# Per-chunk waits in the FFN groups, statistics straight from fp32 x, and PSUM banks of their own for the LayerNorm broadcasts

## The chip, the cores and the metric

The kernel runs on one Trainium2 chip, the same program on all 8 NeuronCores, each on its own batch element of 2048 tokens. No core talks to another. The time is that of the slowest core, in microseconds (us).

## What is computed

A macaron layer: half an FFN, attention, half an FFN, each on a LayerNorm of x and added back to x. The model width is 1024. The FFN is one shared expert and two routed ones, all with a hidden width of 4096; a token goes to one routed expert by argmax of a two-row gate.

```python
def _L0_attn_ref(x, wq, bq, wu, bu):          # 16 heads of 64
    q = x @ wq.T + bq
    qh = q.reshape(HEADS, b, s, hd)           # keys and values are qh too
    attn = softmax(qh @ qh^T * scale)
    return (attn @ qh).reshape(b, s, emb) @ wu.T + bu

def _L0_ffn_ref(x, ...):
    top1 = argmax(softmax(xf @ gate_w.T))
    masked = xf * one_hot(top1)               # one copy per routed expert
    routed = sum_e(relu(masked_e @ w1_e + b1_e) @ w2_e + b2_e)
    shared = relu(xf @ sw1 + sb1) @ sw2 + sb2
    return routed + shared

x = x + 0.5 * ffn(layernorm(x))
x = x + attn(layernorm(x))
x = x + 0.5 * ffn(layernorm(x))
```

## The kernel before

x lies transposed and in fp32 in `x_sb` (128 partitions, 8 chunks `kc` of the width, 2048 tokens) for the whole run. Tokens are cut into 4 strips `st` of 512. The hidden width of the three experts is cut into 12 pieces `sup` of 1024: 0 to 3 are the shared expert (class 0), 4 to 7 and 8 to 11 the routed ones (classes 1 and 2). The loop is over `sup`, within it over `st`: each of these 48 steps of an FFN, called a step below, is `do_mm1` and then `do_mm2` (L535, L578). The weights of the next `sup` are fetched by the POOL queue into the other of two slots.

`do_mm1` makes 8 groups `hc` of 8 matmuls (L552) in turn into PSUM banks `ps_a` and `ps_b`; ScalarE takes each group through ReLU into its part of `ar_h` (L562). The right-hand side is the LayerNorm output `ar_ln` for class 0, and for the routed classes a masked copy `ar_b` of 8 chunks. The 8 masked chunks of the next step are made by VectorE (L524), one behind each of the 8 evacuations of the present `do_mm2` (`pending_lnm`). `do_mm2` makes 8 groups `dc` of 8 matmuls (L586) in turn into `ps_c` and `ps_d`; VectorE adds each to `x_sb` (L606, for `sup` 0 L599).

Each engine runs its instructions in the order in which the program emits them. Order between engines is kept by counting semaphores, one per producing engine: `sch.wait("tensor", DVE, n)` holds everything behind it on TensorE until VectorE has done n counted operations. Before the change, the first matmul of `do_mm1` waits for all 8 chunks, and the first of `do_mm2` for all 8 parts of `ar_h` (`h_all`).

LayerNorm works by strip in two stages. `stage_stats` (L308): VectorE casts a chunk of x to bf16 into a one-strip scratch (L325), TensorE sums it over partitions by a matmul with a column of ones (L333, one output row), 8 times in turn through that one scratch; then ScalarE squares a chunk into the same scratch (L347) and TensorE sums it (L355), 8 times in turn; VectorE writes both rows (L340, L362). `stage_post` (L367): on one row, variance (L377, L379), square root on ScalarE (L386), reciprocal (L391); TensorE spreads both rows over 128 partitions with two fp32 matmuls (L400, L404), VectorE copies them out (L410, L412) and normalises 8 chunks with two operations each (L422, L426), through the scratch. `stage_gate` (L432) makes the routing masks.

In an FFN these stages are written into the steps of `sup` 0: stats 0, stats 1, post 0, then for each strip `do_mm1`, stats of strip st+2, post of strip st+1, `do_mm2`, and the gates from strip 2 on. `do_mm2` of `sup` 0 waits for all that VectorE has been given so far (`mm2_extra`), because the broadcasts and gates use `ps_c` and `ps_d` too; `ext["bc_wait"]` guards the same banks from the other side. In attention, `emit_ln` (L492) writes stats 0, stats 1, post 0, stats 2, post 1, stats 3, post 2, post 3; then `qproj` (L895) waits for all of it (`ln_done`).

Of the kernel before, what the change touches and what calls it, by code (L numbers as in the profile page):

```python
# [12 lines left out]
NT = 2048  # L13
# [55 lines left out]
def build(phases=("ffn1", "attn", "ffn2")):  # L69
# [15 lines left out]
    with es:  # L85
# [14 lines left out]
        ones_col = sb("ones_col", [128, 1], BF16)  # L100
        onesLf = sb("onesLf", [1, 128], F32)
# [188 lines left out]
        def make_ln_stages(is_ffn, xwaits, statps, bcps, ext=None):  # L290
# [7 lines left out]
            bcev = [0] * NSTRIP  # L298

# [8 lines left out]
            def stage_stats(st):  # L308
                t0 = st * TS
                xb = scratch(st)  # L310
# [4 lines left out]
                sch.wait("vector", DVE, max(xwaits[st], tok_b2))  # L315
                sch.wait("scalar", DVE, max(xwaits[st], tok_b2))
                prev_mm = statmm[st - 1] if st > 0 else 0
                sch.wait("vector", X, tok_xload)
                if st >= 2:
                    sch.wait("vector", DVE, ln_tok[st - 2])  # L320
                for kc in range(NKC):
                    sch.wait("vector", MM, prev_mm)
                    sch.wait("vector", ACTs, sqtok[st - 2] if st >= 2 else 0)
                    def fcast(v, S, _kc=kc, _t0=t0, _xb=xb):
                        v.tensor_copy(  # L325
                            _xb[:, :], x_sb[:, _kc * NT + _t0: _kc * NT + _t0 + TS]
                        ).then_inc(S[DVE], 1)
                    sch.emit("vector", fcast)
                    ctok = sch.bump(DVE, 1)
                    sch.wait("tensor", GP, tok_gpinit)  # L330
                    sch.wait("tensor", DVE, max(ctok, s1ev[st - 1] if st >= 1 else 0))
# [6 lines left out]
                sch.wait("vector", MM, s1mm)  # L338
                def fs1(v, S, _sp=sp1, _r=r1):
                    v.tensor_scalar_mul(_r, _sp, 1.0 / D).then_inc(S[DVE], 1)  # L340
                sch.emit("vector", fs1)
                s1ev[st] = sch.bump(DVE, 1)
                for kc in range(NKC):
                    sch.wait("scalar", MM, prev_mm)
                    sch.wait("scalar", X, tok_xload)
# [7 lines left out]
                    sch.wait("tensor", DVE, s2ev[st - 1] if st >= 1 else 0)  # L353
# [4 lines left out]
                    prev_mm = sch.bump(MM, 1)  # L358
                statmm[st] = prev_mm
# [7 lines left out]
            def stage_post(st):  # L367
# [34 lines left out]
                bct1 = sch.bump(MM, 1)  # L402
                def fbc2(t, S, _r=r2, _bp=bB):
# [11 lines left out]
                xb = scratch(st)  # L415
                sch.wait("vector", DVE, bcev[st])
                sch.wait("vector", ACTs, sqtok[st])
                for kc in range(NKC):
                    base_n = sch.val(DVE)
                    def fn(v, S, _kc=kc, _t0=t0, _b=base_n, _xb=xb, _mB=mB, _sB=sB):  # L420
                        v.wait_ge(S[DVE], _b)
                        v.tensor_sub(_xb[:, :],  # L422
# [3 lines left out]
                        v.tensor_mul(ln_ap(_kc, _t0, TS), _xb[:, :],  # L426
                                     _sB[:, :]).then_inc(S[DVE], 1)
                    sch.emit("vector", fn)
                    ln_tok[st] = sch.bump(DVE, 2)


            def stage_gate(st):  # L432
# [4 lines left out]
                for e in range(2):  # L437
                    gp_ps = bcps[e]
                    for kc in range(NKC):
                        sch.wait("tensor", *tok_gw)  # L440
                        sch.wait("tensor", DVE, ln_tok[st])
                        sch.wait("tensor", DVE, ext.get("bc_wait", 0))
# [14 lines left out]
                    gevac = sch.bump(DVE, 1)  # L457
                sch.wait("vector", DVE, gevac)
# [9 lines left out]
                sch.wait("tensor", DVE, mrow_tok)  # L468
                bB2 = bcps[1]
# [15 lines left out]
                mask_tok[st] = sch.bump(DVE, 2)  # L485

# [17 lines left out]
        def emit_ffn(xwait_dve, wst, ps_d, ps_w, ps_w2):  # L504
            ext = {"bc_wait": 0}
# [8 lines left out]
            lnm_tok = [None]  # L514

            pending_lnm = []

            def build_lnm_pieces(st, klass, wait_mm):
                which = 0 if klass == 1 else 1
                def piece(kc):  # L520
# [6 lines left out]
                    lnm_tok[0] = sch.bump(DVE, 1)  # L527
                return [lambda _kc=kc: piece(_kc) for kc in range(NKC)]
# [6 lines left out]
            def do_mm1(sup, st, klass, slot):  # L535
# [80 lines left out]
            for st in range(NSTRIP):  # L616
                do_mm1(0, st, 0, 0)
                ext["bc_wait"] = sch.val(DVE)
# [12 lines left out]
            for st in (2, 3):  # L631
                ext["bc_wait"] = sch.val(DVE)
                gf[st]()
            ps2_free[0] = ps2_free[1] = sch.val(DVE)
# [18 lines left out]
        def emit_attn(xwait_dve, s0, s1, d_att, ps_t, ps_rz, hooks):  # L653
# [106 lines left out]
            def av_row(i, a):  # L760
                if a == 0:
                    sch.wait("tensor", DVE, state["avfree"])
# [132 lines left out]
            def qproj(half):  # L895
                t0h = half * 1024
                qev = [0, 0]
                for dc in range(NKC):
                    for st2 in range(2):
# [3 lines left out]
                        sch.wait("tensor", DVE, max(ln_done, state["avfree"],  # L903
# [67 lines left out]
        if do1:  # L971
            with nc.psum_tensor("ps_d1", [128, TS], F32) as ps_d1, \
                 nc.psum_tensor("ps_w1", [1, TS], F32) as ps_w1, \
                 nc.psum_tensor("ps_v1", [1, TS], F32) as ps_v1:
# [11 lines left out]
                xw, _, ffn1_mm = emit_ffn(0, wst1, ps_d1, ps_w1, ps_v1)  # L986
# [26 lines left out]
        if do2:  # L1013
            with nc.psum_tensor("ps_d2", [128, TS], F32) as ps_d2, \
                 nc.psum_tensor("ps_w2", [1, TS], F32) as ps_w2, \
                 nc.psum_tensor("ps_v2", [1, TS], F32) as ps_v2:
# [13 lines left out]
                _, xtok, _ = emit_ffn(xw, wst2, ps_d2, ps_w2, ps_v2)  # L1030
# [97 lines left out]
```

## Time and profile before

| what | us |
|---|---|
| median of the 2 runs shown | 4909.22 (4900.01 to 4918.43) |
| the profiled execution, its own time | 4656.95 |
| its span on the slowest core (core 6) | 4655.4 |
| the other cores' spans | 4630.0 to 4653.5 |
| FFN 1, attention, FFN 2 within the span | about 50 to 1731, 1731 to 2980, 2980 to the end |

The profiled execution is 252 us shorter than the median of the runs. Busy time of TensorE matmuls on core 6 is 3826.6 us (82%), of VectorE 1235.9 us (27%), of ScalarE 1221.7 us (26%). In the rows, PE is TensorE, PEld its weight loads, DVE VectorE, ACT ScalarE. PEclk or "clock" is the granted TensorE clock as a share of full speed. A row of the timeline gives start, duration, engine, line, operation, output<-inputs, a count, and in brackets the idle time before it and what ended that. The end of the last matmul of a merged row is modelled: a row of 8 lasts 1.89 us, while the next begins 1.73 us after its start.

### The profile page before, as it was taken

Reading aid. Unit: us, or ns where it says so; the run is one execution under the profiler, and the core shown is the slowest. Engines: PE = TensorE matmul, PEld = TensorE weight load, DVE = VectorE, ACT = ScalarE, POOL = GpSimd, SP = SyncE. Lnnn points to the kernel's source line nnn. Section 1 sums busy time; section 2 is a strip of 40 time slices with the busy share of each in tenths; the row PEclk is TensorE's granted clock in tenths of the full one; section 3 lists DMA queues with packets and bytes.
Section 4 is the critical chain, followed back from the end, with each engine's and each line's share of the span. In section 5 each row is a group of like instructions: output and inputs, shape, how many; then the busy total and the mean of one; then the engine's idle time right before and its main releaser. Section 6 shows DMA issues by size and latency. Waiting matters only on the chain. (4 is left out here: it accounts for less than half of the span.)

```text
span 4655.4 us, 45328 instructions; the slowest of 8 cores (4630.0 to 4655.4 us)
## 1 busy us (share of the span) xinstructions
PE 3826.6 (82%) x16529; PEld 1583.2 (34%) x16784; DVE 1235.9 (27%) x2311; ACT 1221.7 (26%) x2945; POOL 48.5 (1%) x66
## 2 busy tenths in 40 slices
PE   1568999999999983588888888655899999999998
PEld 0223444444444430123333333222344444444443
DVE  2342112222222224411222222234211222222222
ACT  1111111111111111266664666311111111111111
POOL 0000000000000000000000000000000000000000
PEclk9778899999999995656566656667999999999999
DMA  7002222222221100100001000300222222222101
GB/s 145 0 0 37 37 37 37 37 37 37 37 35 30 28 1 0 18 1 1 1 1 19 1 1 1 55 0 0 37 37 37 37 37 37 37 37 32 30 12 73
DMA packets 55268, 124.61 MB, mean 27 GB/s; under 512 B 1808, under 2 KB 1808, under 8 KB 53008
## 3 DMA queue, kind: packets, MB, share of 16 engines
q0 software_dynamic: 52144, 104.86, 14.6%
q1 hardware_dynamic: 2912, 16.85, 1.1%
q8 instruction: 142, 2.33, 0.2%
q14 instruction: 70, 0.57, 0.0%
HBM read 218.18 MB, written 8.39 MB: 49 GB/s over the span
## 5 line engine op out<-in xcount | busy, mean ns | idle before, releaser
L586 PE MATMUL ps_c<-ar_h,ar_w 128*128 128x512 bf16 x3009 | 735.9, 385 | 177.3 <-DVE ar_ln L426 88.2
L562 ACT ACTIVATE ar_h<-ps_a,b1hf 128x512 bf16<-128x512 f32 x384 | 263.8, 687 | 2188.7 <-PE ps_a L552 2188.7
L586 PE MATMUL ps_d<-ar_h,ar_w 128*128 128x512 bf16 x3012 | 729.7, 383 | 3.3
L606 DVE TENSOR_TENSOR x_sb<-x_sb,ps_c 128x512 f32<-128x512 f32 x352 | 242.0, 687 | 1712.4 <-PE ps_c L586 1712.4
L552 PE MATMUL ps_a<-ar_b,ar_w 128*128 128x512 bf16 x2010 | 482.0, 380 | 88.8 <-DVE ar_b L524 86.9
L586 PEld LDWEIGHTS ps_c<-ar_h,ar_w 128*128 128x128 bf16 x3072 | 297.1, 99 | 575.4 <-issue 256.3
L552 PE MATMUL ps_b<-ar_b,ar_w 128*128 128x512 bf16 x2004 | 480.7, 380 | 2.3
L741 PE MATMUL s<-ar_h 64*128 64x512 bf16 x768 | 413.9, 566 | 74.8 <-ACT ar_w L752 54.5
L586 PEld LDWEIGHTS ps_d<-ar_h,ar_w 128*128 128x128 bf16 x3072 | 303.2, 99 | 371.5 <-issue 29.1
L562 ACT ACTIVATE ar_h<-ps_b,b1hf 128x512 bf16<-128x512 f32 x384 | 263.8, 687 | 412.6 <-PE ps_b L552 410.8
L752 ACT ACTIVATE ar_w<-s 128x512 bf16<-128x512 f32 x432 | 255.0, 599 | 285.7 <-PE s L741 285.2
L606 DVE TENSOR_TENSOR x_sb<-x_sb,ps_d 128x512 f32<-128x512 f32 x352 | 242.0, 688 | 288.6 <-PE ps_d L586 288.6
L552 PEld LDWEIGHTS ps_a<-ar_b,ar_w 128*128 128x128 bf16 x2048 | 196.1, 98 | 343.9 <-issue 117.8
L552 PEld LDWEIGHTS ps_b<-ar_b,ar_w 128*128 128x128 bf16 x2048 | 200.8, 98 | 242.8 <-issue 2.1
L552 PE MATMUL ps_a<-ar_ln,ar_w 128*128 128x512 bf16 x993 | 252.8, 396 | 31.9 <-DVE rzb_sb L325 14.9
L552 PE MATMUL ps_b<-ar_ln,ar_w 128*128 128x512 bf16 x1011 | 251.1, 391 | 0.6
L524 DVE TENSOR_TENSOR ar_b<-ar_ln,ar_b 128x512 bf16<-128x512 bf16 x512 | 212.8, 418 | 0.0
L741 PEld LDWEIGHTS s<-ar_h 64*128 64x128 bf16 x768 | 74.8, 103 | 363.0 <-issue 361.9
L552 PEld LDWEIGHTS ps_a<-ar_ln,ar_w 128*128 128x128 bf16 x1024 | 102.9, 101 | 163.1 <-issue 63.9
L741 PE MATMUL ps_t<-ar_h 64*128 64x512 bf16 x256 | 147.8, 577 | 4.8
L552 PEld LDWEIGHTS ps_b<-ar_ln,ar_w 128*128 128x128 bf16 x1024 | 103.0, 101 | 129.8 <-issue 29.7
L752 ACT ACTIVATE ar_ln<-s 128x512 bf16<-128x512 f32 x176 | 105.3, 614 | 42.8 <-PE s L741 42.8
(172 smaller groups left out, 2533.5 us busy)
## 6 DMA issues: line engine op xcount, KB each, us to landing
ar_w<-w1c POOLq DMA_DIRECT2D x24, 2048.0 KB, 18.1
ar_w<-w2c POOLq DMA_DIRECT2D x24, 2048.0 KB, 29.0
x_sb<-x SPq DMA_DIRECT2D x1, 8192.0 KB, 37.8
y<-x_sb SPq DMA_DIRECT2D x8, 1024.0 KB, 8.7
ar_w<-wqt POOLq DMA_DIRECT2D x1, 2048.0 KB, 16.7
ar_w<-wut POOLq DMA_DIRECT2D x1, 2048.0 KB, 16.4
b1hf<-b1h SPq DMA_DIRECT2D x1, 48.0 KB, 39.8
bq_sb<-bqc SPq DMA_DIRECT2D x1, 4.0 KB, 40.9
```

Source lines behind the costliest of these rows:

```text
L524: v.tensor_mul(lnm_ap(_kc), ln_ap(_kc, _st * TS, TS), mask_ap(_w, _st)).then_inc(S[DVE], 1)
L552: ins = t.matmul(_pst[:, :], w1blk(_slot, _kc, _hc), _rhs(_kc), start=(_kc == 0), stop=(_kc == NKC - 1))
L562: s.activation(ar_h[:, _hc * TS:(_hc + 1) * TS], _pst[:, :], AF.Relu, bias=b1hf[:, _sup * 8 + _hc:_sup * 8 + _hc + 1], scale=0.5).then_inc ...
L586: ins = t.matmul(_pst[:, :], w2blk(_slot, _hc, _dc), ar_h[:, _hc * TS:(_hc + 1) * TS], start=(_hc == 0), stop=(_hc == NKC - 1))
L606: v.tensor_add(xsl, xsl, _pst[:, :]).then_inc(S[DVE], 1)
L741: t.matmul(_sr[:, :], qq_ap(_pa, _h), ar_h[_h:_h + 64, _q4 * TS:(_q4 + 1) * TS], start=True, stop=True).then_inc(S[MM], 1)
L752: s.activation(prow_ap(_a)[:, _q4 * TS:(_q4 + 1) * TS], _sr[:, :], AF.Exp, scale=SCALE, accum_out=_z[:, _a * 4 + _q4:_a * 4 + _q4 + 1]).th ...
```

## The change

- The sum of x is taken by fp32 matmuls directly from `x_sb` with a column of fp32 ones; the 8 casts of a strip and their waits go.
- The squares alternate between two scratch tiles (`xb_s`, `xb2`), each with its own wait.
- Normalisation writes straight into `ar_ln` and scales it there; the scratch is not used. Each chunk's count is kept (`ln_ktok`), and so is each masked chunk's (`lnm_ktok`).
- The first group of `do_mm1` waits chunk by chunk, and the first group of `do_mm2` waits part by part of `ar_h`.
- The FFN's broadcasts and gates get two banks of their own, `ps_e` and `ps_f`, each with its own release (`bfree`). `bc_wait` and the wait of `sup` 1 for the gates go. `mm2_extra` stays.
- `qproj` waits for the strip it reads, and `av_row` takes over the wait for all of LayerNorm.

```diff
@@ stage_stats
-                xb = scratch(st)
...
-                prev_mm = statmm[st - 1] if st > 0 else 0
-                sch.wait("vector", X, tok_xload)
-                if st >= 2:
-                    sch.wait("vector", DVE, ln_tok[st - 2])
+                sch.wait("tensor", GP, tok_gpinit)
+                sch.wait("tensor", X, tok_xload)
+                sch.wait("tensor", DVE, max(xwaits[st], tok_b2,
+                                            s1ev[st - 1] if st >= 1 else 0))
                 for kc in range(NKC):
-                    sch.wait("vector", MM, prev_mm)
-                    sch.wait("vector", ACTs, sqtok[st - 2] if st >= 2 else 0)
-                    def fcast(v, S, _kc=kc, _t0=t0, _xb=xb):
-                        v.tensor_copy(
-                            _xb[:, :], x_sb[:, _kc * NT + _t0: _kc * NT + _t0 + TS]
-                        ).then_inc(S[DVE], 1)
-                    sch.emit("vector", fcast)
-                    ctok = sch.bump(DVE, 1)
...
-                    def fmm(t, S, _kc=kc, _sp=sp1, _xb=xb):
-                        t.matmul(_sp, ones_col[:, :], _xb[:, :],
+                    def fmm(t, S, _kc=kc, _t0=t0, _sp=sp1):
+                        t.matmul(_sp, ones_colf[:, :],
+                                 x_sb[:, _kc * NT + _t0: _kc * NT + _t0 + TS],
                                  start=(_kc == 0), stop=(_kc == NKC - 1)).then_inc(S[MM], 1)
...
                 for kc in range(NKC):
-                    sch.wait("scalar", MM, prev_mm)
-                    sch.wait("scalar", X, tok_xload)
+                    xb = xb_s if kc % 2 == 0 else xb2
+                    sch.wait("scalar", MM, sq_mm_last[kc % 2])
...
+                    sq_mm_last[kc % 2] = prev_mm
@@ stage_post
-                sch.wait("tensor", DVE, ext.get("bc_wait", 0))
-                if st >= 1:
-                    sch.wait("tensor", DVE,
-                             mask_tok[st - 1] if is_ffn else bcev[st - 1])
+                sch.wait("tensor", DVE, bfree[0])
...
+                sch.wait("tensor", DVE, bfree[1])
...
-                        v.tensor_sub(_xb[:, :],
+                        v.tensor_sub(ln_ap(_kc, _t0, TS),
                                      x_sb[:, _kc * NT + _t0: _kc * NT + _t0 + TS],
                                      _mB[:, :]).then_inc(S[DVE], 1)
                         v.wait_ge(S[DVE], _b + 1)
-                        v.tensor_mul(ln_ap(_kc, _t0, TS), _xb[:, :],
+                        v.tensor_mul(ln_ap(_kc, _t0, TS), ln_ap(_kc, _t0, TS),
                                      _sB[:, :]).then_inc(S[DVE], 1)
...
+                    ln_ktok[st][kc] = ln_tok[st]
@@ emit_ffn
-                (ps_w[:, :], ps_w2[:, :]), (ps_d[:, :], ps_c[:, :]), ext)
+                (ps_w[:, :], ps_w2[:, :]), (ps_e[:, :], ps_f[:, :]), ext)
@@ do_mm1
-                    sch.wait("tensor", rhs_sem, rhs_tok)
+                    if hc > 0:
+                        sch.wait("tensor", rhs_sem, rhs_tok)
                     for kc in range(NKC):
+                        if hc == 0:
+                            sch.wait("tensor", rhs_sem, rhs_ktok[kc])
@@ do_mm2
-                    sch.wait("tensor", ACTs, h_all)
+                    if dc > 0:
+                        sch.wait("tensor", ACTs, h_all)
                     for hc in range(NKC):
+                        if dc == 0:
+                            sch.wait("tensor", ACTs, h_relu_tok[hc])
@@ emit_ffn, after sup 0
-            ps2_free[0] = ps2_free[1] = sch.val(DVE)
@@ qproj
-                        sch.wait("tensor", DVE, max(ln_done, state["avfree"],
+                        sch.wait("tensor", DVE, max(ln_tok[half * 2 + st2],
+                                                    state["avfree"],
                                                     state["ufree"]))
```

How the instructions move is shown at two places. First TensorE in a step of a routed class, from the last group of one `do_mm2` (ps_d) through `do_mm1` (ps_a, ps_b) to the first group of its `do_mm2` (ps_c). Before:

```order
L586 MATMUL ps_d<-ar_h,ar_w 128x512 [waits s_dve]
L586 MATMUL ps_d<-ar_h,ar_w 128x512 x7
L552 MATMUL ps_a<-ar_b,ar_w 128x512 [waits s_dve]
L552 MATMUL ps_a<-ar_b,ar_w 128x512 x7
L552 MATMUL ps_b<-ar_b,ar_w 128x512 x8
...
L552 MATMUL ps_b<-ar_b,ar_w 128x512 x7
L586 MATMUL ps_c<-ar_h,ar_w 128x512 [waits s_act]
L586 MATMUL ps_c<-ar_h,ar_w 128x512 x7
```

The same place in the changed kernel:

```order
L599 MATMUL ps_d<-ar_h,ar_w 128x512 [waits s_dve]
L599 MATMUL ps_d<-ar_h,ar_w 128x512 x7
L562 MATMUL ps_a<-ar_b,ar_w 128x512 x5
L562 MATMUL ps_a<-ar_b,ar_w 128x512 [waits s_dve] x3
L562 MATMUL ps_b<-ar_b,ar_w 128x512 x8
...
L562 MATMUL ps_b<-ar_b,ar_w 128x512 x7
L599 MATMUL ps_c<-ar_h,ar_w 128x512 x6
L599 MATMUL ps_c<-ar_h,ar_w 128x512 [waits s_act] x2
```

Five matmuls of `do_mm1` now stand ahead of the first wait for VectorE (the waits of those five are already covered by an earlier one), and six of `do_mm2` ahead of the first wait for ScalarE; the matmuls themselves and their order are unchanged.

Second TensorE in stats 0 and the first of stats 1 of the first FFN (ps_w takes the sums of x, ps_v those of the squares; rzb_sb and p_ex are the two scratch tiles). Before:

```order
L333 MATMUL ps_w<-rzb_sb,ones_col 1x512 [waits s_gp,s_dve]
L333 MATMUL ps_w<-rzb_sb,ones_col 1x512 [waits s_dve] x7
L355 MATMUL ps_v<-rzb_sb,ones_col 1x512 [waits s_act] x8
L333 MATMUL ps_w<-p_ex,ones_col 1x512 [waits s_dve] x8
L355 MATMUL ps_v<-p_ex,ones_col 1x512 [waits s_act] x8
```

And in the changed kernel:

```order
L326 MATMUL ps_w<-x_sb,ones_colf 1x512 [waits s_gp,s_x,s_dve]
L326 MATMUL ps_w<-x_sb,ones_colf 1x512 x7
L353 MATMUL ps_v<-rzb_sb,ones_col 1x512 [waits s_act]
L353 MATMUL ps_v<-p_ex,ones_col 1x512 [waits s_act]
...
L326 MATMUL ps_w<-x_sb,ones_colf 1x512 [waits s_dve]
L326 MATMUL ps_w<-x_sb,ones_colf 1x512 x7
```

The 8 sums of x have one wait at their head instead of one each and read `x_sb`; the sums of the squares keep a wait each but alternate between the two scratch tiles.

## Rows read from the trace of the kernel before

**Rows 1.** the page: busy time, share of the span and instructions of each engine

```profile
PE 3826.6 (82%) x16529; PEld 1583.2 (34%) x16784; DVE 1235.9 (27%) x2311; ACT 1221.7 (26%) x2945; POOL 48.5 (1%) x66
```

**Rows 2.** waits, core 6: who waited for whom, us in total, times, longest

```profile
PE ps_c L586 <- DVE ar_ln L426: 88.2, 6, 14.9
PE ps_a L552 <- DVE ar_b L524: 86.9, 64, 3.6
PE ps_c L586 <- ACT ar_h L562: 85.9, 90, 1.4
```

**Rows 3.** timeline, one step of class 1: TensorE, VectorE, ScalarE

```profile
3764.41 1.89 PE L586 MATMUL ps_d<-ar_h,ar_w 128*128 128x512 bf16 x8
3767.57 1.89 PE L552 MATMUL ps_a<-ar_b,ar_w 128*128 128x512 bf16 x8 [1.28 <-DVE ar_b L524]
3779.66 1.89 PE L552 MATMUL ps_b<-ar_b,ar_w 128*128 128x512 bf16 x8
3782.47 1.89 PE L586 MATMUL ps_c<-ar_h,ar_w 128*128 128x512 bf16 x8 [0.93 <-ACT ar_h L562]
...
3766.40 0.69 DVE L606 TENSOR_TENSOR x_sb<-x_sb,ps_d 128x512 f32<-128x512 f32 x1 [0.71 <-PE ps_d L586]
3767.01 0.42 DVE L524 TENSOR_TENSOR ar_b<-ar_ln,ar_b 128x512 bf16<-128x512 bf16 x1
...
3781.64 0.69 ACT L562 ACTIVATE ar_h<-ps_b,b1hf 128x512 bf16<-128x512 f32 x1 [1.04 <-PE ps_b L552]
```

**Rows 4.** timeline, first LayerNorm of FFN 1: stats and post of strip 0

```profile
50.66 0.58 PE L333 MATMUL ps_w<-rzb_sb,ones_col 128*1 128x512 bf16 x1 [50.66 <-DVE rzb_sb L325]
...
71.85 0.68 DVE L362 TENSOR_SCALAR ar_b<-ps_v 1x512 f32<-1x512 f32 x1 [10.95 <-PE ps_v L355]
...
94.19 0.68 DVE L362 TENSOR_SCALAR p_ex<-ps_v 1x512 f32<-1x512 f32 x1 [10.95 <-PE ps_v L355]
...
100.76 2.04 PE L400 MATMUL ps_d<-ar_b,onesLf 1*128 1x512 f32 x2 [6.68 <-DVE ar_b L391]
102.60 1.91 PE L404 MATMUL ps_c<-ar_b,onesLf 1*128 1x512 f32 x2
...
119.05 3.57 PE L552 MATMUL ps_a<-ar_ln,ar_w 128*128 128x512 bf16 x8 [14.54 <-DVE ar_ln L426]
```

**Rows 5.** timeline, TensorE where class 1 begins

```profile
3668.53 1.89 PE L586 MATMUL ps_d<-ar_h,ar_w 128*128 128x512 bf16 x8
3674.04 3.57 PE L552 MATMUL ps_a<-ar_b,ar_w 128*128 128x512 bf16 x8 [3.62 <-DVE ar_b L524]
```

**Rows 6.** timeline, TensorE and VectorE: stats 2 in FFN 1

```profile
134.91 0.38 PE L333 MATMUL ps_w<-rzb_sb,ones_col 128*1 128x512 bf16 x1
...
155.04 0.68 DVE L362 TENSOR_SCALAR ar_b<-ps_v 1x512 f32<-1x512 f32 x1 [10.95 <-PE ps_v L355]
```

**Rows 7.** timeline, TensorE: the gate of strip 2 in FFN 1

```profile
371.05 3.57 PE L444 MATMUL ps_d<-ar_ln,gw_bf 128*1 128x512 bf16 x8 [1.74 <-DVE ar_b L483]
374.41 2.50 PE L444 MATMUL ps_c<-ar_ln,gw_bf 128*1 128x512 bf16 x8
```

**Rows 8.** timeline, TensorE and VectorE: LayerNorm of attention

```profile
1732.34 0.38 PE L333 MATMUL s<-rzb_sb,ones_col 128*1 128x512 bf16 x1 [2.06 <-DVE rzb_sb L325]
...
1776.72 0.68 DVE L362 TENSOR_SCALAR p_ex<-s 1x512 f32<-1x512 f32 x1 [10.95 <-PE s L355]
...
1823.29 0.68 DVE L362 TENSOR_SCALAR ar_b<-s 1x512 f32<-1x512 f32 x1 [10.95 <-PE s L355]
...
1919.46 2.87 PE L908 MATMUL ps_a<-ar_ln,ar_w 128*128 128x512 bf16 x7 [14.92 <-DVE ar_ln L426]
```

**Rows 9.** windows, core 6: busy us of PE, PEld, DVE, ACT, POOL, granted clock, DMA

```profile
400.00:500.00 100.00, 96.50 (x362) 39.85 (x369) 16.52 (x24) 15.11 (x22) 0.00 (x0) 0.81 0.21 34
800.00:900.00 100.00, 92.91 (x420) 41.45 (x428) 24.54 (x48) 20.31 (x30) 1.76 (x2) 1.00 0.11 16
```

**Rows 10.** the same view, core 0

```profile
400.00:500.00 100.00, 95.81 (x436) 43.04 (x444) 19.94 (x29) 18.34 (x27) 0.00 (x0) 1.00 0.18 27
```

More of the change, by code:

```diff
@@ L100, in build @@
         ones_col = sb("ones_col", [128, 1], BF16)
+        ones_colf = sb("ones_colf", [128, 1], F32)
         onesLf = sb("onesLf", [1, 128], F32)
@@ L184, in g_init @@
             g.memset(ones_col[:, :], 1.0)
+            g.memset(ones_colf[:, :], 1.0)
             g.memset(onesLf[:, :], 1.0)
@@ L298, in make_ln_stages @@
             bcev = [0] * NSTRIP
+            bfree = [0, 0]
+            sq_mm_last = [0, 0]
+            ln_ktok = [[0] * NKC for _ in range(NSTRIP)]
+            ext["ln_ktok"] = ln_ktok
             def tiles(st):
@@ L338, in stage_stats @@
                 sch.wait("vector", MM, s1mm)
+                sch.wait("vector", DVE, ln_tok[st - 2] if st >= 2 else 0)
                 def fs1(v, S, _sp=sp1, _r=r1):
@@ L342, in stage_stats @@
                 s1ev[st] = sch.bump(DVE, 1)
+                sch.wait("scalar", DVE, max(xwaits[st], tok_b2))
+                sch.wait("scalar", X, tok_xload)
                 for kc in range(NKC):
-                    sch.wait("scalar", MM, prev_mm)
-                    sch.wait("scalar", X, tok_xload)
+                    xb = xb_s if kc % 2 == 0 else xb2
+                    sch.wait("scalar", MM, sq_mm_last[kc % 2])
                     def fsq(s, S, _kc=kc, _t0=t0, _xb=xb):
@@ L352, in stage_stats @@
                     sch.wait("tensor", ACTs, sqtok[st])
-                    sch.wait("tensor", DVE, s2ev[st - 1] if st >= 1 else 0)
+                    if kc == 0:
+                        sch.wait("tensor", DVE, s2ev[st - 1] if st >= 1 else 0)
                     def fmm2(t, S, _kc=kc, _sp=sp2, _xb=xb):
@@ L414, in stage_post, with fn @@
                 bcev[st] = sch.bump(DVE, 2)
-                xb = scratch(st)
+                bfree[0] = bcev[st] - 1
+                bfree[1] = bcev[st]
                 sch.wait("vector", DVE, bcev[st])
-                sch.wait("vector", ACTs, sqtok[st])
                 for kc in range(NKC):
                     base_n = sch.val(DVE)
-                    def fn(v, S, _kc=kc, _t0=t0, _b=base_n, _xb=xb, _mB=mB, _sB=sB):
+                    def fn(v, S, _kc=kc, _t0=t0, _b=base_n, _mB=mB, _sB=sB):
                         v.wait_ge(S[DVE], _b)
-                        v.tensor_sub(_xb[:, :],
+                        v.tensor_sub(ln_ap(_kc, _t0, TS),
                                      x_sb[:, _kc * NT + _t0: _kc * NT + _t0 + TS],
@@ L441, in stage_gate @@
                         sch.wait("tensor", DVE, ln_tok[st])
-                        sch.wait("tensor", DVE, ext.get("bc_wait", 0))
+                        sch.wait("tensor", DVE, bfree[e])
                         def fg(t, S, _e=e, _kc=kc, _t0=t0, _sp=gp_ps):
@@ L457, in stage_gate @@
                     gevac = sch.bump(DVE, 1)
+                    bfree[e] = gevac
                 sch.wait("vector", DVE, gevac)
@@ L468, in stage_gate @@
                 sch.wait("tensor", DVE, mrow_tok)
+                sch.wait("tensor", DVE, max(bfree[0], bfree[1]))
                 bB2 = bcps[1]
@@ L485, in stage_gate @@
                 mask_tok[st] = sch.bump(DVE, 2)
+                bfree[0] = mask_tok[st] - 1
+                bfree[1] = mask_tok[st]
             stats_fns = [lambda _st=st: stage_stats(_st) for st in range(NSTRIP)]
@@ L502, in emit_ln, with emit_ffn @@
             return ln_tok, mask_tok
-        def emit_ffn(xwait_dve, wst, ps_d, ps_w, ps_w2):
-            ext = {"bc_wait": 0}
+        def emit_ffn(xwait_dve, wst, ps_d, ps_w, ps_w2, ps_e, ps_f):
+            ext = {}
             sf, pf, gf, ln_tok, mask_tok = make_ln_stages(
                 True, [xwait_dve] * NSTRIP,
-                (ps_w[:, :], ps_w2[:, :]), (ps_d[:, :], ps_c[:, :]), ext)
+                (ps_w[:, :], ps_w2[:, :]), (ps_e[:, :], ps_f[:, :]), ext)
+            ln_ktok = ext["ln_ktok"]
             h_relu_tok = [0] * NKC
@@ L514, in emit_ffn @@
             lnm_tok = [None]
+            lnm_ktok = [0] * NKC
             pending_lnm = []
@@ L542, in do_mm1 @@
                     rhs = lambda kc, _t0=st * TS: ln_ap(kc, _t0, TS)
+                    rhs_ktok = [ln_ktok[st][kc] for kc in range(NKC)]
                 else:
@@ L545, in do_mm1 @@
                     rhs = lambda kc: lnm_ap(kc)
+                    rhs_ktok = list(lnm_ktok)
                 for hc in range(NKC):
@@ L761, in av_row @@
                 if a == 0:
-                    sch.wait("tensor", DVE, state["avfree"])
+                    sch.wait("tensor", DVE, max(state["avfree"], ln_done))
                 sch.wait("tensor", ACTs, state["exp_tok"][(i, a, 3)])
@@ L973, in build @@
                  nc.psum_tensor("ps_w1", [1, TS], F32) as ps_w1, \
-                 nc.psum_tensor("ps_v1", [1, TS], F32) as ps_v1:
+                 nc.psum_tensor("ps_v1", [1, TS], F32) as ps_v1, \
+                 nc.psum_tensor("ps_e1", [128, TS], F32) as ps_e1, \
+                 nc.psum_tensor("ps_f1", [128, TS], F32) as ps_f1:
                 for s0 in range(2):
@@ L1015, in build @@
                  nc.psum_tensor("ps_w2", [1, TS], F32) as ps_w2, \
-                 nc.psum_tensor("ps_v2", [1, TS], F32) as ps_v2:
+                 nc.psum_tensor("ps_v2", [1, TS], F32) as ps_v2, \
+                 nc.psum_tensor("ps_e2", [128, TS], F32) as ps_e2, \
+                 nc.psum_tensor("ps_f2", [128, TS], F32) as ps_f2:
                 if wst2["w1"][0] is None:
```

14 lines of the change are left out of this document (3 added, 11 removed).

## The prediction

> **What bounds the kernel now.** I read the page first. TensorE is busy for 82% of the span, no other engine for more than 27% [rows 1]. A kernel like that gains only where TensorE stands still or runs at a lower clock, so the second view is the list of waits, cut down to those of TensorE [rows 2]. Three lines stand out, and the change aims at two. 85.9 us go in 90 waits of the first group of `do_mm2` for the ReLU on ScalarE, 86.9 us in 64 waits of the first group of `do_mm1` for the masked chunks of VectorE. The third, 88.2 us in 6 waits of about 14.7 us, is `do_mm2` of `sup` 0 waiting until the next strip is normalised.
>
> The third view is the timeline of one step [rows 3]. Groups of 8 matmuls begin 1.73 us apart, 0.216 us a matmul. The last `ps_d` group begins at 3764.41, so the next group could begin at 3766.14; it begins at 3767.57, 1.43 us late. In between stand the evacuation of `ps_d` (from 3766.40, 0.69 us) and the eighth masked chunk (3767.01, 0.42 us, done at 3767.43). The last `ps_b` group begins at 3779.66, its follower could begin at 3781.39 and begins at 3782.47, 1.08 us late, behind a ReLU that ends at 3782.33. All the earlier chunks and parts were ready long before. That is 2.5 us beside 128 x 0.216 = 27.6 us of matmuls, a step of 30.2.
>
> LayerNorm is the rest. In the first one TensorE's first sum begins at 50.66 and the second row of strip 0 is written at 71.85, that of strip 1 at 94.19: 21.8 us (from the cast that starts 0.6 before 50.66) and 22.3 us for the statistics of a strip of 512 tokens. In them one scratch tile is passed to and fro between engines. Post of strip 0 ends where the first group begins, at 119.05, about 24.2 us after that second row [rows 4].
>
> **Step 1, the first group of `do_mm2`.** The wait for all eight parts becomes one per part. The eighth matmul would start 7 x 0.216 = 1.51 us after 3781.39, at 3782.90, and its part is ready at 3782.33, plus the 0.14 us that the hand-over to 3782.47 took. The other seven cover it with 0.4 us to spare. Gain 1.08 x 90 = 97 us [rows 2, 3]. Below this, the idle time itself bounds it, 86 us.
>
> **Step 2, the first group of `do_mm1`.** Of the 64 waits, 62 are as in [rows 3]. The eighth matmul would start at 3766.14 + 1.51 = 3767.65, the chunk is handed over at 3767.57. This cover is thin: 0.08 us. A matmul that has waited starts right behind its weight load, which could cost up to one place of 0.216 us. I take 0.05 us: 62 x 1.38 = 86 us, between 75 and 89. The other two are where a class begins with nothing prepared [rows 5]: TensorE is 3.78 us late (3670.26 to 3674.04), and its first group then takes 3.57 us at the half clock. With waits by chunk that group ends soon after the last chunk. 2 x 4 = 8 us, at least 2.
>
> **Step 3, statistics in the FFNs.** 8 casts and 8 hand-overs go; 8 fp32 matmuls on 128 partitions come, which the trace does not show. The nearest rows are the fp32 broadcasts: 102.60 - 100.76 = 1.84 us for one with 512 columns [rows 4]. That was at the half clock: the group of 8 bf16 matmuls behind it lasts 3.57 us in place of the 1.89 of [rows 3]. At full clock I estimate half of that, 0.92 us. So a pass of 8 is 14.7 us at the half clock and 7.4 at full. Dense matmuls with a single output row ran while the clock rose: 8 of them took 3.36 us from 371.05, and the next 8 last 2.50 us [rows 7]. So behind an idle stretch I take a value between the ends, nearer the fast one: 9.3 us. The squares now run in two tiles; two are ready when the fp32 pass ends, and the other six come at ScalarE's pace, at most the 0.69 us of a ReLU of the same size [rows 3] and 0.1 of hand-over, about 5.3 us to the second row. That is 14.6 us for strips 0 and 1 against 21.8 and 22.3: 7 + 7.5. Strips 2 and 3 follow a warm `do_mm1`: 7.4 + 5.3 = 12.7 us against 155.04 - 134.91 = 20.1 [rows 6]: 7.4 each. The first `do_mm1` follows normalisation chunk by chunk and its group of 3.57 us shrinks to one matmul's length: 3 us. Together 32 us an FFN, 65 for both. If the fp32 pass stays at the half clock it is 14.7 + 5.8 = 20.5 us a strip, and of the 65 only 10 are left. Upper end 70. The other part of the LayerNorm chain is not shortened: `do_mm2` still waits for everything given to VectorE, so the 88 us of the third line in [rows 2] stay. Writing into `ar_ln` in place has the same two operations as before and costs nothing.
>
> **Step 4, LayerNorm of attention.** Before, the casts of strip 2 stood on VectorE behind the normalisation of strip 0, so nothing overlapped: 46.6 us a strip (1823.29 - 1776.72), and 188 us in all from a cast about 0.4 us before 1732.34 to 1919.46 [rows 8]. Now statistics need VectorE for two rows only. Stats of strips 2 and 3 run on TensorE and ScalarE while VectorE normalises. A post stage is 46.6 - 22.3 = 24.3 us, as in the FFN. New sum: 13 + 14.6 for the first two statistics, 4 x 24.3, and 2 x 1.6 for the rows of the other two: 128 us. Gain 60. With a slow fp32 pass the statistics (20.5 us) no longer fit behind a post stage, of which some 14.5 us are left after its broadcasts: 41 + 97 + 12 = 150, gain 38. `qproj` may start its first two groups before the last strip is done; two PSUM banks and VectorE, busy normalising, hold it there, so I count nothing and keep 4 us for the upper end.
>
> **Step 5, banks of their own.** The gates no longer wait for the mask copies of the one before (1.74 us idle at 371.05 [rows 7]). About 1 us for each of 8 gates: 8 us, from 4 to 12.
>
> **Sum.** 97 + 86 + 8 + 65 + 60 + 8 = 324 us. The profiled execution took 4656.95, so its like would take 4333. The median of the runs is 4909.22, 252 us more; the removed waits are fixed hand-overs between engines, so I take the same 324 off: 4585. From the bounds, 4560 to 4690.
>
> **Rival A, the clock gives it back (slower).** Core 6 ran 400 to 500 at a granted clock of 0.81, neither of the two levels of 1.2 and 2.4 GHz, while core 0 on the other die had 1.00 with the same work [rows 9, 10]. It fell in the densest stretch (96.5 us busy of 100), and was 1.00 where every step had the wait for the masked chunks (92.9). The change makes all steps as dense as that. At 0.81 a matmul takes 0.216/0.81 = 0.266 us, 0.05 more. Two FFNs have 2 x 48 x 128 = 12,288 of them: 614 us, less some 30 that core 6 has already paid, 584. The gain is gone once 324/0.05 = 6,500 matmuls, 53%, run so. The time would be 4657 - 324 + 584 = 4917 if the 252 us above the profile are already this, and 5169 if they are not. Against it: core 0 was as dense and kept 1.00, and both kernels pass through the dense stretch.
>
> The Trainium skill, TensorE: Matmul & The Clock Gate, section Seeing it yourself, says that a peak-current limit takes a die to 13/16 of the clock when three of its cores run dense matmuls, and holds it while the load lasts. By that rule both kernels should be held there in all of the FFNs. The trace shows the level (0.81) but not the rule: only for a part of the time and on part of the cores.
>
> **Rival B, fp32 passes stay slow and the eighth wait binds.** All lower ends: 97 + 75 + 2 + 10 + 38 + 4 = 226 us, 4683. For it: the first sum lasts 0.58 us where the first of stats 2, behind dense work, lasts 0.38 [rows 4, 6], so sparse statistics leave the clock low.
>
> **Rival C, the runs fall to the profile's level.** The same gain at the clock of the profiled execution: 4335. For it speaks only that the profiled execution was there.
>
> **Rival D, the waits move and don't shrink.** Then the change does not do what it says: waits one by one stop TensorE as long as one wait did, steps 1 and 2 give nothing, and 65 + 60 + 8 + 8 = 141 us are left: 4768. Against it, [rows 3]: the earlier chunks are ready before the group begins.
>
> **How the numbers follow.** The forecast has 0.62, A 0.12, B 0.14, C 0.08, D 0.04. A measurement of this kernel tells about 2% from no change, that is 98 us. The forecast, B, C and D are all faster by more than that, 0.88; of A I put 0.07 within 2% and 0.05 slower; I give the first 0.87 and the middle 0.08. The range leaves out A and C and holds the rest with the mixed cases between: 4400 to 4850.
>
> **What would show it.** In the profile after: the two waits of [rows 2] at under 10 us each, and routed steps of 27.7 us instead of 30.2. If steps stay over 29 us, step 2 is wrong. An fp32 sum's pitch near 0.92 us within stats of strips 2 and 3 confirms step 3; 1.84 there means B. In attention, `qproj` should begin about 130 us after the last evacuation of FFN 1. A granted clock near 0.81 in the routed steps, on more than half of the FFN time, means A, and then the time misses upwards though every wait is gone.

## The result and the profile after

| | before | changed |
|---|---|---|
| median of all runs | 4721.57 (10 runs, 4634.19 to 5054.93) | 4551.65 (11 runs, 4289.92 to 4801.87) |
| undisturbed runs, mean of 5 | 4648.5 (4634.2 to 4658.6) | 4308.8 (4289.9 to 4314.2) |
| profiled execution, its span | 4656.95, 4655.4 | 4315.33, 4313.7 |

The changed kernel is faster: ratio 0.9269, 95% interval 0.9235 to 0.9304, in undisturbed runs 340 us. "Undisturbed" leaves out the runs in which the cores of one die, at times of both, were granted a lower clock and took longer (in one run of the changed kernel cores 0 to 3 had 0.76 and took up to 4827 us, cores 4 to 7 had 0.867 and took at most 4289). Forecast were 324 us of gain, a time of 4585 and a range from 4400. The gain is right to 5%, the time is not: the undisturbed time lies 276 us below the forecast and 90 below the range.

The page, busy time of each engine:

```profile
PE 3842.3 (89%) x16880; PEld 1602.4 (37%) x16880; DVE 1194.8 (28%) x2215; ACT 1217.3 (28%) x2945; POOL 48.5 (1%) x67
```

TensorE's busy time is within 16 us of that in [rows 1]; the span shrank around it. VectorE lost 41 us, the casts. The waits on core 7, the slowest (us in total, times, longest):

```profile
PE ps_c L599 <- DVE ar_ln L423: 87.6, 6, 14.9
```

and the group of the page that holds the waits of `do_mm1` (busy, mean ns, idle before it):

```profile
L562 PE MATMUL ps_a<-ar_b,ar_w 128*128 128x512 bf16 x2048 | 485.8, 379 | 2.8 <-DVE ar_b L528 2.6
```

Of the three lines of [rows 2] the one for `ar_ln` stays at 6 waits and 88 us. The one for masked chunks fell from 86.9 to 2.6 us, and `ps_c` has none for `ar_h` any more. One step of a routed class, core 7, the place that answers to [rows 3]:

```profile
3484.44 1.89 PE L599 MATMUL ps_c<-ar_h,ar_w 128*128 128x512 bf16 x8
...
3496.52 1.89 PE L599 MATMUL ps_d<-ar_h,ar_w 128*128 128x512 bf16 x8
3498.25 1.89 PE L562 MATMUL ps_a<-ar_b,ar_w 128*128 128x512 bf16 x8
...
3510.34 1.89 PE L562 MATMUL ps_b<-ar_b,ar_w 128*128 128x512 bf16 x8
3512.06 1.89 PE L599 MATMUL ps_c<-ar_h,ar_w 128*128 128x512 bf16 x8
...
3498.52 0.69 DVE L619 TENSOR_TENSOR x_sb<-x_sb,ps_d 128x512 f32<-128x512 f32 x1 [0.35 <-PE ps_d L599]
3499.13 0.42 DVE L528 TENSOR_TENSOR ar_b<-ar_ln,ar_b 128x512 bf16<-128x512 bf16 x1
```

From `ps_c` to `ps_c` 27.62 us, which is 128 x 0.216 and nothing more. The last chunk is made while the group that reads it already runs: it ends at 3499.55, which with the hand-over of 0.14 us of the prediction makes 3499.69, and the eighth matmul is due at 3498.25 + 1.51 = 3499.76.

LayerNorm of FFN 1, TensorE on core 0, the place of [rows 4]:

```profile
48.37 10.00 PE L326 MATMUL ps_w<-x_sb,ones_colf 128*1 128x512 f32 x16 [48.37 <-DVE b2sh L241]
58.21 0.38 PE L353 MATMUL ps_v<-rzb_sb,ones_col 128*1 128x512 bf16 x1
...
62.68 7.03 PE L326 MATMUL ps_w<-x_sb,ones_colf 128*1 128x512 f32 x16
69.55 0.38 PE L353 MATMUL ps_v<-rzb_sb,ones_col 128*1 128x512 bf16 x1
...
80.86 2.04 PE L396 MATMUL ps_e<-ar_b,onesLf 1*128 1x512 f32 x2 [6.67 <-DVE ar_b L390]
...
149.48 3.57 PE L599 MATMUL ps_c<-ar_h,ar_w 128*128 128x512 bf16 x8 [14.54 <-DVE ar_ln L423]
```

The 8 fp32 sums (16 records) take 9.84 us from 48.37 and 6.87 from 62.68, the 8 squares behind them 4.47. The broadcasts begin 32.5 us after the first sum; before they began 50.1 us after it [rows 4]. The last row is one of the six waits that stay.

Attention's LayerNorm, TensorE on core 0 and one row of VectorE, the place of [rows 8]:

```profile
1571.82 7.03 PE L326 MATMUL s<-x_sb,ones_colf 128*1 128x512 f32 x16 [1.27 <-PEq L1057]
...
1601.54 2.04 PE L396 MATMUL ps_c<-ar_b,onesLf 1*128 1x512 f32 x2 [6.67 <-DVE ar_b L390]
...
1605.22 9.82 PE L326 MATMUL s<-x_sb,ones_colf 128*1 128x512 f32 x16
...
1618.99 0.69 DVE L423 TENSOR_TENSOR ar_ln<-ar_ln,ar_b 128x512 bf16<-128x512 bf16 x1
1619.14 0.38 PE L353 MATMUL s<-p_ex,ones_col 128*1 128x512 bf16 x1
...
1676.72 2.04 PE L396 MATMUL ps_c<-p_ex,onesLf 1*128 1x512 f32 x2 [20.27 <-DVE p_ex L390]
...
1680.80 3.19 PE L916 MATMUL ps_a<-ar_ln,ar_w 128*128 128x512 bf16 x7 [0.33 <-issue]
1683.78 2.97 PE L916 MATMUL ps_b<-ar_ln,ar_w 128*128 128x512 bf16 x8
1696.04 3.57 PE L916 MATMUL ps_a<-ar_ln,ar_w 128*128 128x512 bf16 x8 [9.28 <-DVE ar_b L925]
```

The sums of strip 2 (from 1605.22) run while VectorE normalises strip 0, so the post stages, 25 us apart, set the pace. They only just do: the last sum of squares of strip 2 starts at 1619.14, and the last operation of the normalisation ends at 1618.99 + 0.69 = 1619.68. Longer statistics would show. Two groups of `qproj` are made while the last strip is normalised, and the third waits for an evacuation behind that.

Core 0 of both profiled executions, cut at the first matmul of each part:

| part | before | changed | difference |
|---|---|---|---|
| FFN 1, LayerNorm and class 0 | 688.4 | 636.6 | -51.9 |
| FFN 1, routed classes | 968.3 | 886.9 | -81.4 |
| attention, LayerNorm and qproj | 217.4 | 151.3 | -66.0 |
| attention, the rest | 1032.3 | 1031.5 | -0.8 |
| FFN 2, LayerNorm and class 0 | 693.3 | 630.2 | -63.1 |
| FFN 2, routed classes | 981.3 | 899.5 | -81.8 |

These add to 345 us on core 0 (spans 4630.0 and 4284.3).

### The profile page after: what moved, and what is told of

It is laid out like the page before. It is cut to its first block and busy times, and to the rows that moved or that the text cites. A ratio compares the mean times of both kernels' runs of the same rounds, so it can differ in the third digit from the quotient of the medians.

```text
span 4313.7 us, 45734 instructions; the slowest of 8 cores (4284.3 to 4313.7 us)
## 1 busy us (share of the span) xinstructions
PE 3842.3 (89%) x16880; PEld 1602.4 (37%) x16880; DVE 1194.8 (28%) x2215; ACT 1217.3 (28%) x2945; POOL 48.5 (1%) x67
## 5 line engine op out<-in xcount | busy, mean ns | idle before, releaser
L599 PE MATMUL ps_c<-ar_h,ar_w 128*128 128x512 bf16 x3072 | 741.5, 385 | 87.6 <-DVE ar_ln L423 87.6
```

Of the source, the lines that this page charges most:

```text
L599: ins = t.matmul(_pst[:, :], w2blk(_slot, _hc, _dc), ar_h[:, _hc * TS:(_hc + 1) * TS], start=(_hc == 0), stop=(_hc == NKC - 1))
```

## The experiments

The time of an experiment is that of its fastest run, beside the fastest run of its reference on the same chip; the fastest two or three runs of one kernel mostly lie within 4 us of each other. "Theory" in the expectations is the sum of the prediction at the lower level, with its terms by part.

### One part alone

`e1_mm2_only` is the kernel before with the waits of `do_mm2` split:

```diff
-                    sch.wait("tensor", ACTs, h_all)
+                    if dc > 0:
+                        sch.wait("tensor", ACTs, h_all)
                     for hc in range(NKC):
+                        if dc == 0:
+                            sch.wait("tensor", ACTs, h_relu_tok[hc])
```

> Step 1 alone on the kernel before: the first group of do_mm2 waits part by part. If the eighth ReLU is covered by seven matmuls, the 90 waits of 1.08 us go and no other wait grows: 97 us less than before, routed steps of 29.1 us. Rival (the waits only move): the ReLU wait reappears before the eighth matmul or in front of do_mm1, and the time stays within 10 us of before.

Measured: 4541.4 against 4635.4, 94 us off, ratio 0.9798 (0.9769 to 0.9826); a routed step takes 29.06 us on core 0, where the kernel before takes 30.15. Its waits on core 0:

```profile
PE ps_c L589 <- DVE ar_ln L426: 88.0, 6, 14.9
PE ps_a L552 <- DVE ar_b L524: 86.8, 64, 3.6
```

Exactly one line of [rows 2] is gone and the other two are unchanged: the idle time was removed, not moved.

`e2_mm1_only` is the kernel before with the same edit in `do_mm1` (and the counts it needs):

```diff
-                    sch.wait("tensor", rhs_sem, rhs_tok)
+                    if hc > 0:
+                        sch.wait("tensor", rhs_sem, rhs_tok)
                     for kc in range(NKC):
+                        if hc == 0:
+                            sch.wait("tensor", rhs_sem, rhs_ktok[kc])
```

> Step 2 alone on the kernel before: the first group of do_mm1 waits chunk by chunk. If the cover of 0.08 us holds: 94 us less than before (62 waits of 1.4 us, two of 4, and up to 3 us in each first do_mm1 behind a LayerNorm: 100). Rival (the eighth wait binds and costs a weight load): 75 to 80 us less, with a gap of about 0.2 us before the eighth matmul in 62 steps.

Measured: 4531.0, 104 us off, ratio 0.9777 (0.9735 to 0.9819). A steady routed step takes 28.72 us on core 0 for 30.15, the whole 1.43 us of the late start, so the thin cover of the eighth matmul holds.

`e3_ln_only` is the changed kernel with both waits put back (the two edits above reversed), so that steps 3 to 5 are alone.

> The changed kernel with both waits of the steps put back, so LayerNorm, gates and banks alone. If the parts add up: what is left of the 340 us between the fast runs after 97 and 94, about 149 us less than before. Rival (the LayerNorm part is worth only my lower ends, 52 us, and the two step waits give more than their price because TensorE keeps its clock): under 100 us less.

Measured: 4488.9, 147 us off, ratio 0.9685 (0.9657 to 0.9713). The three parts add to 94 + 104 + 147 = 345, the whole measured 340 (the means of the first table) to 346 (the fastest runs, on different chips): no interaction shows.

### The statistics

The next three ran beside the changed kernel on another chip (`a1_after_again`, 4289.3).

> The changed kernel once more, as the mark for the other three on this chip: 340 us less than before if the level at which both are compared is that of the undisturbed runs (4649 and 4309), 324 by my sum.

`e7_sums_twice` makes the fp32 sums of every strip twice; `start` restarts the sum, so the output is the same.

```diff
-                for kc in range(NKC):
+                for kc in list(range(NKC)) * 2:
                     def fmm(t, S, _kc=kc, _t0=t0, _sp=sp1):
```

> The changed kernel with every fp32 sum of x made twice (the second time over the same accumulator, so the row is unchanged). It prices the fp32 pass: 8 matmuls of 0.86 us more in each of the 8 strips of the FFNs and the first 2 of attention, 69 us, and 0 to 14 us in the other 2 of attention, which lie beside a normalisation: 70 to 85 us more than the changed kernel. Rival (the pass is hidden behind ScalarE's squares): under 30 us more.

Measured: 4374.7, in a single run, 85 us more. Against the profiled execution of the changed kernel the LayerNorm part of FFN 1 grew on core 0 by 28 us, of FFN 2 by 31 and of attention by 26. TensorE there:

```profile
48.22 15.55 PE L326 MATMUL ps_w<-x_sb,ones_colf 128*1 128x512 f32 x32 [48.22 <-DVE b2sh L241]
...
68.08 13.89 PE L326 MATMUL ps_w<-x_sb,ones_colf 128*1 128x512 f32 x32
```

The second pass costs 13.73 - 6.87 = 6.86 us at full clock, 0.858 us per matmul of 512 columns, 12 times 82 us. All of it is on the path, in attention too, where I had thought that two of the four strips hide it: the rows of attention above show that the statistics of strip 2 end together with the normalisation beside them, so nothing is left to hide a second pass.

`e4_bf16_casts` takes the sums of x from bf16 casts again, but through the two scratch tiles in turn:

```diff
+                    xb = xb_s if kc % 2 == 0 else xb2
+                    sch.wait("vector", MM, sq_mm_last[kc % 2])
...
+                        v.tensor_copy(
+                            _xb[:, :], x_sb[:, _kc * NT + _t0: _kc * NT + _t0 + TS]
...
-                        t.matmul(_sp, ones_colf[:, :],
-                                 x_sb[:, _kc * NT + _t0: _kc * NT + _t0 + TS],
+                        t.matmul(_sp, ones_col[:, :], _xb[:, :],
```

> The changed kernel with the sums of x taken from bf16 casts on VectorE again, but through both scratch tiles in turn. If fp32 is worth having only where it frees VectorE: statistics in the FFNs get a little shorter (8 casts of 0.43 us in place of 8 sums of 0.86, the first squares no longer ready beforehand), about 15 us less over both FFNs, while in attention the casts of strips 2 and 3 stand behind a normalisation again, 20 us more. In all within 20 us of the changed kernel. Rival (fp32 itself is the gain): 40 us or more above it.

Measured: 4304.5, 15 us more; the profiled execution took 4324.4, and on cores 4 to 7 at most 4298. In it the LayerNorm part of FFN 1 is 7 to 16 us shorter on all cores. That of FFN 2 is 629.6 us on cores 4 to 7, where the changed kernel takes 630.2 at its best; on cores 0 to 3 it is 23 to 25 us longer, at a lower granted clock. Attention's is 20 (core 0) to 22 us (cores 5 to 7) longer. Attention, strip 2, core 0:

```profile
1609.84 0.58 PE L334 MATMUL s<-rzb_sb,ones_col 128*1 128x512 bf16 x1 [14.87 <-DVE rzb_sb L327]
...
1615.09 0.58 PE L361 MATMUL s<-rzb_sb,ones_col 128*1 128x512 bf16 x1 [0.44 <-ACT rzb_sb L352]
```

TensorE waits 14.87 us for a cast that stands on VectorE behind a strip's normalisation. So in the FFNs fp32 buys nothing beside the second tile; it pays in attention, because it takes VectorE out of the statistics. The fp32 sums with a single scratch tile were not run. The rows also show the spaced sums at the half clock (0.58 us, where the rows behind an fp32 pass have 0.38).

### The 88 us that stayed

`e5_no_extra` takes away the wait of `do_mm2` of `sup` 0 for everything given to VectorE (`mm2_extra`), which own banks make needless:

```diff
-                do_mm2(0, st, 0, sch.val(DVE))
+                do_mm2(0, st, 0, 0)
```

> The changed kernel without the wait of do_mm2 of sup 0 for all that VectorE was given (mm2_extra). TensorE can then make two groups into ps_c and ps_d while VectorE normalises, and waits for the evacuations after that: 3 to 5 us in each of 6 places, 20 to 30 us less than the changed kernel. Rival (this wait is the whole of the 88 us): 80 us less.

Measured: 4278.4, 11 us less where 20 to 30 were expected. A miss; TensorE on core 0 shows why:

```profile
134.16 3.59 PE L599 MATMUL ps_c<-ar_h,ar_w 128*128 128x512 bf16 x8
137.54 2.90 PE L599 MATMUL ps_d<-ar_h,ar_w 128*128 128x512 bf16 x8
149.43 3.57 PE L599 MATMUL ps_c<-ar_h,ar_w 128*128 128x512 bf16 x8 [8.99 <-DVE x_sb L612]
```

and its waits have, in place of the 87.6 us for `ar_ln`:

```profile
PE ps_c L599 <- DVE x_sb L612: 58.1, 6, 10.2
```

Two groups start early, at the half clock. The third needs `ps_c` back, whose evacuation stands on VectorE behind the normalisation, and after 9 us of idling it is at the half clock too (3.57). So of the 29.5 us of idle time that went, much came back as slow matmuls: here the two groups took 6.3 us (134.16 to 149.43 less 8.99) that take 3.45 at full clock. In the six places 1.8 to 2.8 us were lost so, 13 in all, and the groups behind the wait took 3 us more in all than in the changed kernel. That leaves 13 of 29.5, near the 11 measured.

`e6_post_in_mm1` therefore moves the cause. The row part of post is emitted ahead of `do_mm1` of `sup` 0, its broadcasts and normalisation behind the fourth group of it, and the extra wait goes; in attention the rows of strips 2 and 3 stand ahead of the normalisation of the strip before.

```diff
                     ps1_free[hc % 2] = h_relu_tok[hc]
+                    if inject is not None and hc == 3:
+                        inject()
...
-            sf[0](); sf[1](); pf[0]()
+            sf[0][0](); sf[0][1](); pf[0][0](); sf[1][0](); pf[0][1](); sf[1][1]()
             for st in range(NSTRIP):
-                do_mm1(0, st, 0, 0)
+                if st + 1 < NSTRIP:
+                    pf[st + 1][0]()
+                    do_mm1(0, st, 0, 0, pf[st + 1][1])
...
-                do_mm2(0, st, 0, sch.val(DVE))
+                do_mm2(0, st, 0, 0)
```

> The changed kernel, with the post stage of the next strip moved: its rows ahead of do_mm1 of sup 0, its broadcasts behind that do_mm1's fourth group, its normalisation on VectorE beside the rest; do_mm2 no longer waits for VectorE as a whole; in attention the row work of a strip stands beside the broadcasts of the one before. If the 88 us of waiting of do_mm2 for LayerNorm are only a matter of order, 24 us of exposed post stage go three times in each FFN, with cold groups behind them: 140 us less than the changed kernel, about 480 less than before. Rival (VectorE is then too full: evacuations queue behind the normalisation and TensorE waits for PSUM instead): under 60 us less than the changed kernel.

Measured, beside e1 to e3: 4112.9, ratio to the kernel before 0.8876 (0.8838 to 0.8914), and 176 us less than the changed kernel (4289.3, on another chip), where 140 were expected. On core 0 the class 0 parts of the two FFNs fell by 80 and 72 us (636.6 to 556.8, 630.2 to 558.5), which is the expected gain, and LayerNorm of attention by 23, for which nothing had been counted. The run has both moves and the missing wait together; the split is from the trace. TensorE on core 0, strip 0 of `sup` 0:

```profile
92.59 1.89 PE L576 MATMUL ps_b<-ar_ln,ar_w 128*128 128x512 bf16 x8
94.41 1.12 PE L407 MATMUL ps_e<-p_ex,onesLf 1*128 1x512 f32 x2
95.37 1.02 PE L412 MATMUL ps_f<-p_ex,onesLf 1*128 1x512 f32 x2
96.32 1.90 PE L576 MATMUL ps_a<-ar_ln,ar_w 128*128 128x512 bf16 x8
...
114.46 0.38 PE L358 MATMUL ps_v<-p_ex,ones_col 128*1 128x512 bf16 x1
114.77 1.90 PE L615 MATMUL ps_c<-ar_h,ar_w 128*128 128x512 bf16 x8
```

`do_mm2` begins right behind the squares, where the changed kernel had waited 14.54 us. The broadcasts stand between dense matmuls and cost 0.96 us each, not the 1.84 of [rows 4].

### The cover of the eighth matmul

`e8_chunk_twice` writes each masked chunk twice, the second time once the first is done; the result is the same. Its reference on a third chip is `a2_after_again` (4288.0).

```diff
                         v.tensor_mul(lnm_ap(_kc), ln_ap(_kc, _st * TS, TS),
                                      mask_ap(_w, _st)).then_inc(S[DVE], 1)
+                        v.wait_ge(S[DVE], _b + 1)
+                        v.tensor_mul(lnm_ap(_kc), ln_ap(_kc, _st * TS, TS),
+                                     mask_ap(_w, _st)).then_inc(S[DVE], 1)
```

> The changed kernel once more, as the mark for the run beside it: 4290 to 4315 us if undisturbed, as in its earlier runs. Both theories expect the same of it.

> The changed kernel with every masked chunk made twice by VectorE (same result), so that the eighth is handed over some 0.42 to 0.5 us later in each of the 62 steady do_mm1 steps. Theory: the seven matmuls ahead of it cover the eighth by only about 0.08 us, so nearly all of that shows: 62 x (0.42 - 0.08) = 21 us, with the hand-over between the two writes up to 62 x 0.45 = 28 us more than the changed kernel, and the idle time appears on the eighth matmul of each step. Rival: the cover is wider than the trace let me work out (the evacuation ahead of the chunk begins earlier, or the pipeline hides it), and it costs under 8 us.

Measured: 4331.3, in a single run, 43 us more, above the 28 expected. TensorE on core 0, a steady step and the start of class 1:

```profile
3500.94 1.67 PE L566 MATMUL ps_a<-ar_b,ar_w 128*128 128x512 bf16 x7
3502.91 0.38 PE L566 MATMUL ps_a<-ar_b,ar_w 128*128 128x512 bf16 x1 [0.29 <-DVE ar_b L532]
...
689.98 0.38 PE L566 MATMUL ps_a<-ar_b,ar_w 128*128 128x512 bf16 x1 [1.80 <-DVE ar_b L532]
690.85 0.38 PE L566 MATMUL ps_a<-ar_b,ar_w 128*128 128x512 bf16 x1 [0.49 <-DVE ar_b L532]
...
696.41 3.62 PE L566 MATMUL ps_b<-ar_b,ar_w 128*128 128x512 bf16 x8
```

In the steady step seven matmuls run through and the eighth, due at 3500.94 + 1.51 = 3502.45, starts at 3502.91: 0.46 us late, for a chunk that is handed over 0.52 us later. The cover is thus 0.06 us, and 62 x 0.46 = 28.5 us. Most of the remaining 15 is the two starts of a class, which I had left out: nothing is prepared there, so every matmul waits for its own doubled chunk (0.87 us a matmul), the clock falls to half meanwhile (0.59 us a matmul from the sixth on) and the next group takes 3.62 us. By the second `ps_b` group, at full clock again, TensorE is 6.5 us later than in the changed kernel, 13 us for both classes.

## Why the prediction was right and wrong

**The step that failed is in *Sum*:** "the removed waits are fixed hand-overs between engines, so I take the same 324 off: 4585". The gain was rightly made against the profiled execution (4656.95) and then moved to the median of two runs, 4909.22. The kernel's undisturbed level was the profile's: 5 of its 10 runs lie at 4634 to 4659, and its fastest runs on three further occasions took 4635, 4636 and 4661. The clocks of the two runs at 4900 and 4918 are not on record; two runs of the same kernel that took 4918.4 and 4916.5 beside the experiments had a die, or both, at 0.80 where the fast ones have 0.85, and that is what I take the two for. What I named rival C and gave 0.08, "the same gain at the clock of the profiled execution: 4335", is what came, 26 us too high. The spans of eight cores in the profile, within 0.6% of each other at clocks of 0.851 to 0.856, were the evidence at hand, and I weighed them as nothing. The median of all runs, 4551.65, comes near 4585 by luck: 6 of the 11 runs were disturbed.

Three smaller sums are off. Rival C's 4335 is 4333 by *Sum*. Rival D counts 8 us of step 2 although it takes steps 1 and 2 for nothing (133 us are left, not 141). The upper ends of the terms give 340 us and so 4569, not 4560. None of them moves the result.

**The mechanism, by its terms.**

| step | forecast | measured |
|---|---|---|
| 1, first group of `do_mm2` | 97 | 94 (e1) |
| 2, first group of `do_mm1` | 94 | 104 (e2) |
| 3, 4, 5, LayerNorm and banks | 133 | 147 (e3) |
| whole | 324 | 340 |

*Step 1* was right: 94/90 = 1.04 us a wait for 1.08. *Step 2* was short because the 0.05 us I took off a step for a late eighth matmul were not lost (30.15 - 28.72 = 1.43 us a step, 89 in all; cover 0.06 by e8), and because the 3 us at each first `do_mm1`, which I had put into step 3, belong to this edit. The two starts of a class gave 4.1 us each for 4.

*Step 3*: the cold fp32 pass took 9.84 us for 9.3, but the second, 6.87, where I had 9.3 again; the warm ones 6.87 for 7.4. The squares took 4.5 us behind it for 5.3. So strip 1 took 11.4 us for 14.6, and FFN 2, whose first pass came warm (6.86 us), gained once more. The low end of 10 us, for an fp32 pass at the half clock, is out: e7 measures 0.858 us a matmul. *Step 4*: 66 for 60, by the same shorter statistics and the two early `qproj` groups that I had counted at nothing; `qproj` begins 109 us after the first sum, not 130. *Step 5* is part of e3 and was not measured by itself; a gate's wait fell from 1.74 [rows 7] to 0.94 us, and the waits of all eight from 10.9 to 3.8, which is 7 for 8.

**Rival A did not come.** Windows of the changed kernel, core 7 (PE busy, PEld, DVE, ACT, POOL, granted clock, DMA):

```profile
3000.00:3100.00 100.00, 90.62 (x322) 34.54 (x321) 25.05 (x36) 11.69 (x17) 1.77 (x2) 0.76 0.27 43
3070.00:3165.00 95.00, 95.00 (x364) 39.35 (x362) 16.40 (x24) 15.00 (x22) 0.00 (x0) 0.81 0.22 36
3100.00:3200.00 100.00, 100.00 (x410) 42.76 (x409) 16.49 (x24) 18.57 (x27) 1.76 (x2) 0.88 0.05 8
3200.00:3300.00 100.00, 100.00 (x465) 45.31 (x463) 20.51 (x30) 19.25 (x28) 0.00 (x0) 1.00 0.22 36
3500.00:3600.00 100.00, 100.00 (x465) 45.36 (x464) 26.59 (x52) 22.03 (x32) 1.75 (x2) 1.00 0.27 43
```

The routed steps are now busy all the time, on all eight cores, and the clock granted there is 1.00. Cores 4 to 7 had 0.81 for a part of FFN 2, on core 7 for some 140 us between 3006 and 3166 (the first and third row mix it with other clocks). It cost 22 to 25 us there; cores 6 and 7 had had such a stretch in FFN 1 before [rows 9]. The profiled executions on two other chips had none (spans within 8 us, 4289 and 4288 us).

The Trainium skill, TensorE: Matmul & The Clock Gate, section Seeing it yourself, would have a die with three dense cores held at 13/16 while the load lasts. The trace agrees on the level, 0.81, and not on the holding: all eight cores ran 880 us of routed steps at 1.00.

Whether the longer runs are that limit, and what starts them, these runs leave open, since no trace of one was kept. Denser steps brought hardly more of them: 6 of 11 runs against 5 of 10 before.

**Rival B** fell with e7 (a warm pass runs at full clock) and with the 27.62 us step. Its worry about the eighth matmul was near: 0.06 us of cover is all there is. **Rival D** fell with e1 and e2.

## What to carry to other kernels

Split a wait for a whole buffer into one per piece where the pieces are made at the pace at which they are read: here 94 and 104 us, with no cost in the steady state even where a piece arrives 0.06 us ahead of its reader. A queue in order is worth more attention than an operation's price: a cast that stood behind a normalisation held TensorE for 14.87 us and attention became 20 us longer (e4), and moving stages in the queues (e6) gave 176 us where removing the wait alone (e5) gave 11. When the runs and the profiled execution differ by 5%, ask first which of them had all cores at the usual clock, and forecast from that level, or from both.

## What the runs showed of the hardware

- An fp32 matmul with one output row costs 0.858 us for 512 columns at full clock (e7), 4.0 times the 0.216 of a bf16 one; a pass of 8 begun after 48 us of idling took 9.84 us, a warm one 6.87.
- Behind a dense fp32 pass the clock was at full for the bf16 squares (0.38 us a record) in strip 0 of FFN 1, though they come with gaps of 0.35 to 0.66 us; in strip 1 of attention the last two of the eight took 0.58. Behind sparse bf16 sums the squares of strip 0 of FFN 1 took 0.58 throughout (e4).
- In e5 the last three of two groups of 8 matmuls took 0.38 us each, and after nine idle microseconds the next group was at the half clock again (3.57 us). In e8 the sixth of eight matmuls spaced by 0.87 us was at the half clock (0.59 us).
- A granted clock of 0.81 came and went in the middle of dense matmuls: on core 7 TensorE was busy for 95 of 95 us from 3070 at 0.81, and for 100 of 100 from 3200 at 1.00, while cores 0 to 3 had 1.00 from 3100 on with the same work.
